# Cross-attention and two-expert feed-forward block: another order of the instructions in the prelude and in the loop's bodies

## The reference

```python
x = x + xattn(layernorm(x), ctx, ctx, mask)     # 16 heads of 16; raw reshape to (b, H, -1, DK)
x = x + ffn(layernorm(x))

# xattn
Q, K, V = (t @ W + b, reshaped to heads)
attn = softmax((Q K^T) * mask) / sqrt(16);  out = (attn V) @ Wp + bp
# ffn(x): 8 experts, 0 has W1, b1, W2, b2, and 1 to 7 all have the same perturbed ones
probs = softmax((norm(x) * gamma + beta) @ Wr + br)
out = sum_e probs_e * (gelu(x @ W1_e + b1_e) @ W2_e + b2_e)      # 256 -> 1024 -> 256
# perturb(w): where |w| is in the top 5% w - 0.8 w, where it is in the lowest 5% w + 0.8 w
```

## Time and profile before

| | |
|---|---|
| median of 3 runs | 729.68 us (726.85 to 730.13) |
| the profiled execution | 726.75 us, its span 724.9 us |
| busy in the span: TensorE, weight loads | 664.5 us (92%), 605.1 us |
| busy: VectorE, ACT, POOL | 512.1 (71%), 386.9 (53%), 257.5 us (36%) |
| mean granted clock of TensorE | 0.933 of full |
| chain that ended last, by engine | PE 65%, DVE 19%, issue 5%, SP's queue 4%, DMA 3% |

### The profile page before, as it was taken

One profiled execution on the slowest core, in us unless ns is written; L12 is line 12 of the kernel. 1 busy time (PEld: TensorE's weight loads), 2 busy tenths in 40 slices (PEclk: granted clock), 3 DMA queues, 4 the chain that ended last, 5 costly groups with the idle time before them and its releaser, 6 DMA issues.

```text
span 724.9 us, 15487 instructions
## 1 busy us (share of the span) xinstructions
PE 664.5 (92%) x5555; PEld 605.1 (83%) x5555; DVE 512.1 (71%) x1221; ACT 386.9 (53%) x498; POOL 257.5 (36%) x271
## 2 busy tenths in 40 slices
PE   3767969999999889999999999899999999999996
PEld 3657858989989779989989989898878988888885
DVE  3787786797797889888789869746994445543452
ACT  3444227747747726766674774755643444435442
POOL 2343461573584458277177356345000000000000
PEclk9776577999999979999999999989999999999999
DMA  7996202531731740471471271220200223113321
GB/s 227 153 213 140 47 24 93 103 71 63 143 52 55 149 85 30 126 127 38 116 132 38 88 129 44 88 95 23 88 1 8 81 87 87 29 58 87 87 58 29
DMA packets 131252, 61.52 MB, mean 85 GB/s; under 512 B 104570, under 2 KB 121988, under 8 KB 131204
## 3 DMA queue, kind: packets, MB, share of 16 engines
q1 hardware_dynamic: 121108, 58.33, 33.9%
q10 hardware_dynamic: 10096, 2.56, 1.9%
HBM read 34.64 MB, written 22.03 MB: 78 GB/s over the span
## 4 chain that ended last, share of the span: by engine, by line
PE 65%; DVE 19%; issue 5%; SPq 4%; DMA 3%; ACT 1%; ACTq 0%; DVEq 0%; POOL 0%; POOLq 0%
PE ps_l L357 8%; PE ps_m L683 7%; PE ps_l L359 7%; PE ps_l L358 7%; PE ps_y L357 5%; PE ps_y L358 5%; PE ps_y L359 5%; PE ps_m L769 4%; PE ps_s L651 4%; PE ps_s L671 3%; DVE ind L1503 3%; DVE region_b L1478 2%; PE ps_s L357 2%; PE ps_m L723 2%; PE ps_s L359 2%
## 5 line engine op out<-in xcount | busy, mean ns | idle before, releaser
L1033 ACT ACTIVATE region_b<-ps_l,bias 128x512 f32<-128x512 f32 x128 | 88.0, 687 | 147.6 <-PE ps_l L359 145.3
L1759 DVE TENSOR_TENSOR region_c_lo<-region_b,region_c_hi 128x512 fp32r<-128x512 f32 x72 | 49.7, 692 | 94.1 <-ACT region_c_hi L1036 94.1
L1036 ACT ACTIVATE region_c_hi<-ps_l,bias 128x512 fp32r<-128x512 f32 x128 | 87.5, 684 | 22.8 <-PE ps_y L359 22.8
L1261 POOL TENSOR_TENSOR region_a<-region_a,mx 128x1024 f32<-128x1024 f32 x32 | 61.9, 1937 | 94.6 <-DVE mx L1406 94.6
L1503 DVE TENSOR_SCALAR ind<-key,cand 128x2048 bf16<-128x2048 uint16 x93 | 94.1, 1050 | 0.1
L1287 POOL TENSOR_TENSOR region_c_lo<-region_b,region_c_hi 128x512 fp32r<-128x512 f32 x56 | 78.5, 1404 | 42.9 <-ACT region_c_hi L1036 42.9
L1005 ACT ACTIVATE ind<-key,cand 128x2048 bf16<-128x2048 uint16 x31 | 62.0, 1999 | 49.7 <-DVE cand L1533 42.1
L357 PE MATMUL ps_y<-w_hi,region_c_hi 128*128 128x256 f32 x256 | 76.3, 298 | 1.4 <-DVE region_c_lo L1759 1.4
L683 PE MATMUL ps_m<-vbd,region_a 128*128 128x34 f32 x512 | 69.0, 294 | 6.6 <-DVE on L1416 6.4
L683 PEld LDWEIGHTS ps_m<-vbd,region_a 128*128 128x128 f32 x512 | 67.4, 212 | 7.3 <-issue 7.2
L359 PE MATMUL ps_y<-w_hi,region_c_lo 128*128 128x256 f32 x256 | 73.3, 286 | 0.0
(11 more groups left out here) (223 smaller groups left out, 1733.4 us busy)
## 6 DMA issues: line engine op xcount, KB each, us to landing
qs<-q_scr SPq DMA_DIRECT2D x16, 512.0 KB, 6.0
xa<-in_x SPq DMA_DIRECT2D x8, 512.0 KB, 5.8
q_scr<-qn_lo SPq DMA_DIRECT2D x16, 256.0 KB, 5.3
x<-in_x SPq DMA_DIRECT2D x32, 128.0 KB, 4.0
region_b<-x SPq DMA_DIRECT2D x8, 512.0 KB, 3.2
out_x<-acc SPq DMA_DIRECT2D x32, 128.0 KB, 2.4
acc_scr<-acc SPq DMA_DIRECT2D x7, 514.0 KB, 5.5
acc<-acc_scr SPq DMA_DIRECT2D x7, 514.0 KB, 3.3
```

What stands on the lines that cost most here:

```text
L1033: act.activation(g[:, f % 4, :], ps_l[:, f % 2, :], ACT.Gelu_apprx_tanh, bias=bias[:, e, f:f + 1]).then_inc(s["gelu"].handle, 1)
L1036: act.activation(gs[0][:, f % 4, :], ps_l[:, f % 2, :], ACT.Gelu_apprx_tanh, bias=bias[:, e, f:f + 1]).then_inc(s["g_hi"].handle, 1)
L1261: pool.tensor_tensor(m, m, mx[:, j, :].unsqueeze(2).to_broadcast([P, H, CT]), ALU.subtract).then_inc(s_shifted.handle, 1)
```

## The change

No operation of the computation is added or left out; only the order, the engine of a few operations and the place of some buffers change.

- SP, prelude: the loads of W2 and Wp and the first mask come after the store of the first keys, the second x and the first reload of keys. `kbd` of batch 0 is loaded ahead of `qs`. The load of the queries of batch 1 stands ahead of `bp` and the residual, the second copy of b2 behind the keys of batch 1.
- TensorE, prelude: the queries of batch 1 are made in two halves between the scores of batch 0, in `ps_l` instead of `ps_y`; the counts and totals of steps 0 to 5 stand elsewhere among attention 0 (each step's totals as before in number); the second pair of keys is transposed after the values.
- ACT, prelude: the eight stores of split keys are spread between its operations, instead of all standing ahead of the first probabilities. It normalises x2 of batch 0 (POOL did) and copies the low halfwords of the weights (`lower_halves`; VectorE did). `normalise(1)` now stands directly ahead of the `kbd` loads, the high part of W2 behind them.
- VectorE, prelude: `low_pair(0)` and the second half of the queries come ahead of the statistics of x 1, the keys of W2 go later.
- `below`, a state of the search of 128x8 elements, moves from SBUF to PSUM.
- Bodies: another order on all five engines. For SP only the waits of the values' load are apart.

The changed lines (blocks of TensorE's and VectorE's bodies with what surrounds them, of the rest the changed lines alone):

```diff
-below = sb("below", [P, NS])
+below = ps_m[:, 1, 3 * NS:4 * NS]
...
+key_lower = sem("key_lower")
...
+    if not (isinstance(b, int) and b == 1):
+        load_values(b)
+def load_values(b):
...
-    sp.dma_start(wraw[:, 1].rearrange("p (c d) -> p c d", c=FC), W2.rearrange("(c p) d -> p c d", p=P)).then_inc(ld_w[1], 16)
...
-    sp.dma_start(view(region_a, 3 * DC * D, DC, D), Wp.rearrange("(c p) n -> p c n", p=P)).then_inc(ld_w4[3], 16)
...
-    load_mask(0)
...
+sp.dma_start(wraw[:, 1].rearrange("p (c d) -> p c d", c=FC), W2.rearrange("(c p) d -> p c d", p=P)).then_inc(ld_w[1], 16)
+sp.dma_start(view(region_a, 3 * DC * D, DC, D), Wp.rearrange("(c p) n -> p c n", p=P)).then_inc(ld_w4[3], 16)
+load_mask(0)
...
-load_queries(0)
...
+load_queries(0)
...
+load_queries(1)
...
-sp.dma_start(b2row[:, 0, :], b2.rearrange("(a d) -> a d", a=1).to_broadcast([P, D])).then_inc(ld_b2row, 16)
-load_queries(1)
...
+sp.dma_start(b2row[:, 0, :], b2.rearrange("(a d) -> a d", a=1).to_broadcast([P, D])).then_inc(ld_b2row, 16)
+load_values(1)
...
-sp.wait_ge(key_ready, 8)
+sp.wait_ge(key_lower, 2)
...
-def queries(b, to=ps_s):
+def queries(b, to=ps_s, only=None):
...
-    for m in range(DC):
+    for m in (range(DC) if only is None else only):
...
-        if j == 2 and not first:
+        if j == 3 and not first:
...
-        wait(pe, q_lo, b + 1)
+        pe.wait_ge(v_biased, KC)
...
-    if to is ps_l:
-        pe.wait_ge(k_lo, 2)
...
+        if to is ps_l:
+            pe.wait_ge(k_lo, 2)
...
-        wait(pe, s_masked, b + 1, 4)
+        wait(pe, s_masked, b + 1, 6)
...
-pe.wait_ge(v_biased, KC)
-queries(1, ps_y)
...
-total(0)
+pe.wait_ge(k_biased, KC)
+queries(1, ps_l, (0,))
...
+total(0)
+queries(1, ps_l, (1,))
...
-for s in range(3):
-    count(1, s)
...
-total(1)
+for s in range(3):
+    count(1, s)
...
-pe.wait_ge(kk_in[1], 64)
-turn_pair(1, ps_l, kk).then_inc(k_turned, 1)
+total(1)
...
-pe.wait_ge(proj_lo[3], 1)
...
+pe.wait_ge(kk_in[1], 64)
+wait(pe, q_lo, 1)
+turn_pair(1, ps_l, kk).then_inc(k_turned, 1)
...
-turn_output(0, ps_l)
+turn_output(0, ps_y)
...
+total(3)
+pe.wait_ge(proj_lo[3], 1)
...
-total(3)
+for s in range(3):
+    count(4, s)
...
-for s in range(3):
-    count(4, s)
...
+for s in range(3):
+    count(5, s)
...
-for s in range(3):
-    count(5, s)
+total(5)
...
-total(5)
...
     turn_probs(i, 0, last)
     h(0)
+    count(p, 0)
     if not last:
         turn_queries_input(i + 1)
-    count(p, 0)
     count(p, 1)
+    count(p, 2)
     h(1)
-    count(p, 2)
+    total(p)
+    values(i, 0)
     turn_probs(i, 1, last)
-    values(i, 0)
-    total(p)
+    h(2)
+    c(0, 0)
     if not last:
         queries(i + 1)
-    c(0, 0)
+    c(0, 1)
     values(i, 1)
     turn_probs(i, 2, last)
-    c(0, 1)
-    h(2)
     c(0, 2)
+    h(3)
+    t(0)
     turn_probs(i, 3, last)
     values(i, 2)
-    h(3)
-    t(0)
+    o(0)
+    if not turn:
+        c(1, 0)
+        c(1, 1)
     values(i, 3)
+    o(1)
+    turn_output(i)
+    if turn:
+        c(1, 0)
+        c(1, 1)
+    c(1, 2)
     h(4)
-    turn_output(i)
-    o(0)
-    o(1)
+    t(1)
+    h(5)
     project(i, 0)
     project(i, 1)
-    c(1, 0)
-    h(5)
+    h(6)
     s(0, 0)
-    c(1, 1)
     s(0, 1)
-    h(6)
+    o(2)
+    c(2, 0)
+    o(3)
     s(1, 0)
-    c(1, 2)
     s(1, 1)
     h(7)
-    t(1)
-    o(2)
+    s(2, 0)
+    s(2, 1)
+    o(4)
+    c(2, 1)
+    c(2, 2)
     turn_x2(i)
-    o(3)
-    s(2, 0)
-    c(2, 0)
+    t(2)
+    o(5)
+    s(3, 0)
+    o(6)
+    s(3, 1)
     r(0)
-    c(2, 1)
+    o(7)
     r(1)
-    c(2, 2)
-    s(2, 1)
     r(2)
-    s(3, 0)
-    o(4)
     r(3)
-    o(5)
-    t(2)
-    s(3, 1)
-    o(6)
-    o(7)
...
-def normalise(b):
-    s = ln[0]
+def normalise(b, n=0, dst=xa, src=xa):
+    s = ln[n]
...
-        act.activation(xa[:, t, :], xa[:, t, :], ACT.Identity, bias=shiftby[0][:, t:t + 1],
-                       scale=rstd[0][:, t:t + 1]).then_inc(s["xhat"].handle, 1)
+        act.activation(dst[:, t, :], src[:, t, :], ACT.Identity, bias=shiftby[n][:, t:t + 1],
+                       scale=rstd[n][:, t:t + 1]).then_inc(s["xhat"].handle, 1)
+def store_split_keys(n, *parts):
+    for m in parts:
+        half_rows = slice(HP * (m % 2), HP * (m % 2) + HP)
+        act.dma_start(kh_scr.rearrange("b p (n m k) -> n m p b k", n=2, m=QG)[n, m][:, 1:4],
+                      kT[n][half_rows, m // 2, CT:4 * CT].rearrange("p (b k) -> p b k", k=CT).bitcast(F32)).then_inc(kh_out, 16)
+def lower_halves(n):
+    low_half = wraw[:, n, :].bitcast(U16).rearrange("p (n two) -> p n two", two=2)[:, :, 0]
+    act.activation(key[:, 2 + n, :], low_half, ACT.Copy).then_inc(key_lower, 1)
...
-high_projection(3, wqp[0][:, 1])
...
-act.wait_ge(ld_w[1], 16)
-act.activation(w2s[0][:], wraw[:, 1, :], ACT.Copy).then_inc(w_hi, 1)
-high_queries_input(1)
...
+high_queries_input(1)
+act.wait_ge(ld_w[1], 16)
+act.activation(w2s[0][:], wraw[:, 1, :], ACT.Copy).then_inc(w_hi, 1)
+high_projection(3, wqp[0][:, 1])
...
-first_queries(1, 0, ps_y)
-first_queries(1, 1, ps_y)
+first_queries(1, 0, ps_l)
...
-for n in range(2):
-    for m in range(QG):
-        half_rows = slice(HP * (m % 2), HP * (m % 2) + HP)
-        act.dma_start(kh_scr.rearrange("b p (n m k) -> n m p b k", n=2, m=QG)[n, m][:, 1:4],
-                      kT[n][half_rows, m // 2, CT:4 * CT].rearrange("p (b k) -> p b k", k=CT).bitcast(F32)).then_inc(kh_out, 16)
...
-sum_signs(1, 0)
+first_queries(1, 1, ps_l)
+store_split_keys(0, 0, 1)
...
+store_split_keys(0, 2, 3)
...
+store_split_keys(1, 0, 1)
...
-sum_signs(2, 0)
+sum_signs(1, 0)
...
-high_pair(1, kT[0], ps_l, k_turned, k_hi)
+store_split_keys(1, 2, 3)
...
+sum_signs(2, 0)
+high_pair(1, kT[0], ps_l, k_turned, k_hi)
+high_output(0, ps_y)
...
-high_output(0, ps_l)
-act.wait_ge(key_ready, 8)
+lower_halves(0)
...
+lower_halves(1)
+normalise(0, 1, xh[1], x2)
+sum_signs(5, 0)
...
-sum_signs(5, 0)
...
+    router_exp(i - 1)
...
-    router_exp(i - 1)
...
+    more_gelu(1)
...
-    more_gelu(1)
+    cmp(0)
...
-    cmp(0)
...
+    if not turn:
+        cmp(1)
...
+    if turn:
+        act.wait_ge(key_ready, 14)
+        act.wait_ge(state_ready, NS + 12)
+        cmp(1)
...
-    if turn:
-        act.wait_ge(key_ready, 16)
-        act.wait_ge(state_ready, NS + 12)
-    cmp(1)
+    cmp(2)
...
+    more_gelu(7)
+    if not last:
+        probs(i + 1, 0)
...
-    cmp(2)
-    more_gelu(7)
...
-        probs(i + 1, 0)
...
-rsqrt(0, 2)
...
+rsqrt(0, 2)
...
+shift(1, 0)
...
-normalise(1, 0, x2, 0, 1, 2, 3)
...
-shift(1, 0)
...
-    bias_residual(i, 0)
-    low(0)
-    bias_residual(i, 1)
-    low(1)
-    low(2)
...
-    low(3)
+    bias_residual(i, 0)
+    bias_residual(i, 1)
+    low(0)
+    if more:
+        normalise(0, i + 2, xa, 0)
+    low(1)
...
+    low(2)
...
-        normalise(0, i + 2, xa, 0)
+        normalise(0, i + 2, xa, 1)
+    low(3)
+    if more:
+        normalise(0, i + 2, xa, 2, 3)
...
-    if more:
-        normalise(0, i + 2, xa, 1, 2)
+    low(5)
...
-        normalise(1, i, x2, 0, 1, 2, 3)
-    low(5)
-    router_rsqrt(i)
-    if not last:
+        normalise(1, i, x2, 0, 1)
...
+        normalise(1, i, x2, 2, 3)
...
-    if more:
-        normalise(0, i + 2, xa, 3)
+    router_rsqrt(i)
...
-    dve.tensor_tensor(below[:], below[:], fcnt[:], ALU.max)
+    dve.tensor_tensor(below, below, fcnt[:], ALU.max)
...
-    dve.memset(below[:], 0.0).then_inc(state_ready, 1)
+    dve.memset(below, 0.0).then_inc(state_ready, 1)
...
-    dve.wait_ge(key_ready, 8 + 2 * n)
+    dve.wait_ge(key_lower, 2)
+    dve.wait_ge(key_ready, 6 + 2 * n)
...
-    dve.tensor_tensor(ranks[:], ranks[:], below[:], ALU.subtract).then_inc(state_ready, 1)
+    dve.tensor_tensor(ranks[:], ranks[:], below, ALU.subtract).then_inc(state_ready, 1)
...
-    dve.wait_ge(key_ready, 16)
+    dve.wait_ge(key_ready, 14)
...
+low_queries(0, ps_s, (0,))
...
-low_queries(0, ps_s, (0,))
+low_queries(0, ps_s, (1,))
+low_pair(0, kT, ps_l, k_hi, k_lo)
...
-low_queries(0, ps_s, (1,))
-keys_of(1)
...
-low_pair(0, kT, ps_l, k_hi, k_lo)
...
+keys_of(1)
...
+compares(0, 0)
...
-compares(0, 0)
-low_queries(1, ps_y)
-counts(0)
...
-decide(0)
+counts(0)
...
+decide(0)
+low_queries(1, ps_l)
...
-counts(1)
...
+counts(1)
+normalise_output(0, 1)
...
-normalise_output(0, 1)
-low_pair(1, kT, ps_l, k_hi, k_lo)
-for n in range(2):
-    dve.tensor_copy(key[:, 2 + n, :], halfword(wraw[:, n, :], 0)).then_inc(key_ready, 1)
...
-counts(2)
...
+counts(2)
...
-low_output(0, ps_l)
+low_pair(1, kT, ps_l, k_hi, k_lo)
+low_output(0, ps_y)
...
-add_residual(0, ps_l)
-stats(1, 0, x2)
...
+add_residual(0, ps_l)
+stats(1, 0, x2)
+counts(4)
...
-counts(4)
...
-top_scores(1, 2)
...
-low_x2(0)
+top_scores(1, 2)
+counts(5)
...
-counts(5)
-logits(0)
+low_x2(0)
...
+logits(0)
...
+    top_scores(i, 3)
+    counts(p)
     if not last:
         low_queries_input(i + 1)
-    top_scores(i, 3)
-    counts(p)
     decide(p)
     if turn:
         end_first_round()
-    cmp(0, 0)
+    cmp(0, 0, 1)
+    if not isinstance(i, int) or i + 2 < B:
```

(52 more changed lines are left out.)

## The result

The new kernel takes 718.2 us by the median (716.6 to 718.3, four runs) against 729.9 (726.9 to 734.7) of the kernel before. The ratio is 0.985, with a 95% interval of 0.982 to 0.988. The forecast was 725 (716 to 735): the sign was right, the size was not. A later control of the same kernel gave 714.8 and a ratio of 0.986 (0.982 to 0.991).

A forecast was written before the change was run, and what follows sets the result against it. TensorE bounds ordinary bodies (98% busy), VectorE next; gains only from low clock or waits. Prelude -1, ordinary bodies -5.0, turn +8, body 7 -5.5 sum to -3.5: 723.3 profiled, 726 by the median, stated as 725 (716 to 735).

The forecast's parts named there:

- Prelude, -1: Start to body 1: earlier key store against a fuller load queue gives -1 us (-7 to +5); attention 0 unchanged.
- the added residual goes behind a decide, three compares and a maximum (4.5 us): Prelude, VectorE: residual delayed 4.5 us, yet the x2 transpose stays near 103.6 and body 1 at 115.
- The rival of the clock in the prelude: Filled gaps keep TensorE at full clock from 45 to 115: -8 us more, 717; chance 0.22.
- `below` in PSUM: Search state moved to PSUM: costs nothing in 31 uses, may give 1 us; the skill's figures estimated 2.0 us cost.
- Ordinary bodies, -5.0: Bodies 1, 2, 4, 5, 6: -6 clock falls, -4 projection waits, +2.5 kbd, +2.5 VectorE tail; bounds -10 and 0.
- The projection's 0.8 each: Five ordinary bodies: the wait before the projection for the low attention output goes, -0.8 us each.
- So the falls of bodies 1, 2 and 4 go: -2 each: Longest stretch without a wide matmul becomes 2.8 us instead of 4.3, so half-clock falls vanish, -2 us each.
- the rival that the falls stay: Ordinary bodies: what busy TensorE does doesn't matter, so reordering leaves the clock falls; +2.5 us, 731; chance 0.18.
- The two costs set against the gain: Ordinary bodies: later `kbd` loads and VectorE's tail waits cost 0.5 us a body each, +2.5 and +2.5.
- Turn, +8: Body 3: waits behind key lowering before values 2 (4 to 5), output transposes (3), counts (4); +8 us (+4 to +9.5).
- Body 7, -5.5: Compare ready, so its wait and 8 us of half clock go, x2 earlier; -5.5 us (-7 to -2).
- VectorE as the bound: Rival: blocked compares or in-order waits delay transposes in five bodies, 2 us each; +10, 735; chance 0.20.

The follow-up runs named there:

- e10: New kernel with all twelve query matmuls of batch 1 ahead of the first scores again; body 1 starts at 110.8 us, against 107.2 in the control.
- e14: New kernel with batch 1's queries ahead of the first scores and the added residual ahead of step 4 again; body 1 starts at 115.2 us.
- e13: New kernel with batch 0's added residual and statistics ahead of search step 4's decide, compares and maximum again; body 1 starts at 111.9 us.
- e11: The new kernel unchanged, run as a control; body 1 starts at 107.2 us.
- e7: New kernel with the loads of W2, Wp and the first mask at their old place on SP; first scores 46.2 us, body 1 at 107.7.
- e5: New kernel plus an unused SBUF tile of 32 bytes a partition where `below` stood; expert 1 takes 182.97 us instead of 185.2.
- e1: New prelude with the loop bodies of the kernel before; ratio to the kernel before 0.988 (0.984 to 0.992).
- e2: Prelude of the kernel before with the new loop bodies; ratio to the kernel before 0.991 (0.987 to 0.994).
- e18: New kernel plus unused SBUF tile, router exponential behind the fourth gelu and reordered turn, run as a control; 708.3 us, ratio 0.980.
- e15: e18's kernel with the second step's first two counts moved behind the attention output's transposes in ordinary bodies; 699.6 us, ratio 0.967.
- e16: e18's kernel with output block 0 ahead of values 2 and output block 1 ahead of values 3 in all bodies; ratio 0.994.
- e6: New kernel with batch 7's router exponential behind the last expert's fourth gelu; body 7 to expert 1 takes 70.9 us instead of 80.1.

## Why the prediction was right or wrong

**Prelude, -1 for -9.9.** The step that failed is the line behind the first transpose: "the last values within 0.3 us of before, and body 1 at 115, as now". That transpose came at 53.2, near the 52.9 forecast; the last values began at 73.8 instead of 78.6, and body 1 at 105.3. Two chains were mis-sized:

- The queries of batch 1 were taken to fill 3.04 us of idle time, and nothing to follow from it. By e10 and e14 their place is worth 3.3 us between the transposes of the probabilities and those of the output, and 1.3 before.
- "the added residual goes behind a decide, three compares and a maximum (4.5 us)", and the x2 transpose was to stay near 103.6. It came at 95.7. The forecast counted what stands ahead of the residual, and not what stood behind it. TensorE's counts of step 4 are ahead of its scores and x2's transposes, so the late compares held the whole line: 3.30 us in the kernel before, 4.47 in e13. Putting the compares first costs x2 some time on VectorE and frees TensorE.

The rival of the clock in the prelude had the right size, and at most a part of the cause. From the first scores to body 1, TensorE is busy 54.5 us in e11 and 53.8 before; its idle time fell from 16.4 to 6.1 us. But the 54.5 hold the twelve matmuls of the queries, which stood ahead of this stretch before, and half clock covers 43.5 us of it in e11 (35.5 in the profile after) against 53.1 before. So some clock came back, from 0.62 to 0.64 and 0.70, and nowhere near the full clock of the rival; with the queries ahead again (e10) half clock covers 54.1 us. The loads' order had no effect (e7); the first scores at 45.9, not 43.5, now wait 6.78 us for the queries, whose two loads are issued behind `kbd`:

```profile
35.62 2.53 SPq L516 DMA_DIRECT2D kbd<-kh_scr  x4
38.25 1.30 SPq L446 DMA_DIRECT2D qs<-q_scr  x2
```

**`below` in PSUM, nothing.** Right. Its update has a median of 156 ns before and 165 after over 31 uses, 0.3 us in all. The 65 ns more, estimated from the Trainium skill (VectorE: DVE Perf Modes, the TRN2 errata section), are not there for these 8 columns. The long ones of the earlier trace rows are gone, but a part of them is now in the operation behind it (`half`), whose longest took 1.38 us, beside a POOL operation of 1.9 us as the 1.50 of the earlier trace rows was. Over attention 0 the two lines are these, five times before, six after:

```profile
L1538 DVE TENSOR_TENSOR below<-below,fcnt 128x8 f32<-128x8 f32 x5 | 4.3, 851 | 0.0
L1540 DVE TENSOR_SCALAR half<-half 128x2 f32<-128x2 f32 x5 | 1.4, 276 | 0.0
```

```profile
L1564 DVE TENSOR_SCALAR half<-half 128x2 f32<-128x2 f32 x6 | 2.6, 437 | 0.0
L1562 DVE TENSOR_TENSOR ps_m<-ps_m,fcnt 128x8 f32<-128x8 f32 x6 | 1.0, 164 | 0.0
```

What the forecast did not cost was the room it left in SBUF, 2.2 us (e5).

**Ordinary bodies, -5.0 for -9.9.** The projection's 0.8 each was right, -4. The step that failed is "So the falls of bodies 1, 2 and 4 go: -2 each": they moved. Half clock covers 14.7 us of the five bodies before and 12.5 after, which is 1 us of the 6, and one stretch costs 1.6 us (54.9 for 53.3), not 2. With the old bodies (before, e1) half clock begins in 4 of 10 ordinary bodies, always at T+48 or 49 (the start of body 1 aside). With the new order of these bodies, in the 14 profiles of the changed kernel and e2 to e14 and again in e18, it begins in 39 of 75, always at T+25 to 28. One of the two in the profile after, the same view as the earlier trace rows, in body 5 from T+26 on:

```profile
358.00:360.00 2.00, 2.00 (x25) 2.00 (x22) 1.04 (x3) 1.99 (x4) 0.05 (x1) 1.00 0.28 55
360.00:362.00 2.00, 2.00 (x11) 2.00 (x11) 0.84 (x4) 0.94 (x2) 2.00 (x3) 0.54 1.06 249
```

So the rival that the falls stay holds in number, not in its argument: what TensorE does matters, since order alone sets the place, and e15 has none. If stretches fell on bodies by chance, at 36 free ones in 75, five free bodies would come once in some 40 profiles (an estimate from these counts), and each of the 15 has at least one stretch.

The fault was to look for the longest single run of narrow matmuls, and that run was misread too. The forecast gave 2.8 us for the new order; by its own list counts, values 1, transposes and counts stand together, and they take 3.5 us (body 2 of the profile after, up to 178.25):

```profile
174.74 0.55 PE L774 MATMUL ps_m<-ones_bf,ind 128*128 128x1 bf16 x16
175.16 1.95 PE L688 MATMUL ps_m<-vbd,region_a 128*128 128x34 f32 x16
176.94 1.07 PE L676 MATMUL ps_s<-ident,region_a 128*128 128x128 f32 x8
177.85 0.54 PE L774 MATMUL ps_m<-ones_bf,ind 128*128 128x1 bf16 x16
```

No stretch of any profile begins behind these, at T+17. And e16, where the longest is 2.6 us in the 7 us before, has more half clock. What in the order places the stretches, these runs do not isolate. By the Trainium skill (TensorE: Matmul & The Clock Gate, what's actually happening) it would be idle or busy alone. Here TensorE idles at most 0.1 us in an ordinary body of e15 and of e18, and only e18 has stretches of half clock, so idle or busy does not tell the two apart.

The two costs set against the gain never came: no wait for `kbd` (+2.5) and none in VectorE's tail (+2.5). VectorE is busy 40.5 to 42.8 us instead of 44.8 to 47.4, its compares 834 ns on average instead of 1050. A further 0.9 us a body, which the forecast didn't have, is TensorE's own: 54.2 us of work became 53.3. Over half of it is the 32 matmuls of the scores, 281 ns each instead of 297.

**Turn, +8 for +3.8.** The mechanism was right, and the size was too large: each of the three waits is there (2.8, 2.4, 5.2 for 4 to 5, 3, 4). The sets of keys took 5.1 and 3.9 us where 6.5 and 4.7 were taken from the earlier trace rows. Beside the second set POOL is busy 1.0 of 4.0 us instead of all of the 4.6; beside the first it is busy all the time now and 5.6 of 6.6 us before, so why that one is shorter stays open. The profiled turn was a short one: the same turn took 66.7 to 69.0 in ten other profiles, with 13.7 to 23.9 us at half clock, and the old one 60.8 in e1, so +6 is the fairer figure.

**Body 7, -5.5 for +5.0.** Two steps failed. The first is "After 510.4 nothing is edited." That is true of the code and not of the time: ScalarE's exponential stands first in the last expert and waits for `logits(7)`, which the new order puts last. That is the wait of 5.21 us. The waits of body 7 itself went as forecast, all but 0.4 us, yet with this one TensorE idles 5.7 us in the stage instead of 4.7.

The second is "so neither the wait nor the 8 us at half clock follow". It came back (449 to 459 and 463 to 466), 1.4 us behind a wait of 0.37, and again behind the exponential's: 20.5 us of the stage instead of 6.8 (the forecast read 8). At half speed the 13.7 us more are 6.9 us of work, and so the larger part of the miss in this profile. It is largely chance: in the eleven profiles with this order half clock covers 3.4 to 20.5 us of the stage, and the median, 74.3, is 0.8 under the 75.1 before. In the runs that had as much half clock there as before (6.8 us: e11, e14) the stage takes 73.3, and without the exponential's wait 70.9 (e6). So the edit gave 1.8 us where 5.5 were forecast, and would have given 4 with the exponential placed later.

**VectorE as the bound** was wrong. No ordinary body waits for it.

## What to carry to other kernels

When an instruction is moved on one engine, look at what is queued behind it and its neighbours on the others: two misses were of this kind, the compares behind the residual (4.8 us) and the exponential behind the logits (a wait of 5.2, worth 2.4). An edit at the end of a straight piece of code must be followed into the next one, the loop included, where a table load is paid in every iteration. And a stretch at half clock seen in three bodies of one profile is a place and a chance, not a sum: count it over several profiles before it is put into a forecast, and before a stage of one profile is read as a gain or a loss.

## What was not expected of the hardware

- In an ordinary body with one order a stretch of half clock begins always at the same place (T+25 to 28 in 39 of 75 bodies, T+48 to 49 in 4 of 10), while TensorE is busy. Moving 0.95 us of counts behind the output's transposes left none in the five bodies of the one profile taken.
- A tile of 32 bytes a partition, used or not, makes 1.2% in a loop of matmuls: 276 to 277 or 281 ns each, 183.0 or 185.2 us.
- A VectorE operation took 1.50 us instead of 0.16 beside a POOL operation. Moved to PSUM it takes 0.17 at most, and the one behind it takes up to 1.38 instead of 0.17.
